# A fused attention kernel in which query products, one unit's additions and the probability spread change engines or form

## The reference, cut to what matters

```python
x = x + L0(gn(x))      # gn: group norm over 32 groups of 4 channels
x = x + L1(gn(x))

# L0: four dilations (1, 2, 4, 8), 32 channels and 2 heads each
q, k, v = split(w_qkv @ x)                          # per dilation i
attn = softmax(sum_d q * unfold3x3(k, dil) * scale) # over 9 neighbours
o = sum_9(attn * unfold3x3(v, dil))
out = concat(o_i * gate_i)     # gate: softmax of a linear layer on pooled x

# L1: 4 heads of 32 channels; p = W_qkv @ x + b, q = k = v = p
att = softmax(p_h @ p_h.T * scale)
out = W_proj @ (att @ p_h) + b_proj
```

## Time and profile before

| | us |
|---|---|
| median of three runs | 90.77 |
| lowest, highest | 90.47, 90.90 |
| span of the profiled execution | 88.6 |

### The profile page before, as it was taken

One profiled execution on the slowest core, in us unless ns is written; L12 is line 12 of the kernel. 1 busy time (PEld: TensorE's weight loads), 2 busy tenths in 40 slices (PEclk: granted clock), 3 DMA queues, 4 the chain that ended last, 5 costly groups with the idle time before them and its releaser, 6 DMA issues.

```text
span 88.6 us, 2254 instructions
## 1 busy us (share of the span) xinstructions
PE 71.5 (81%) x896; PEld 55.5 (63%) x896; DVE 74.1 (84%) x193; ACT 33.9 (38%) x104; POOL 45.6 (52%) x82
## 2 busy tenths in 40 slices
PE   0299997999967899295998799995998098999970
PEld 0299784576425797193988677794876054766840
DVE  1278399999999969999699888999999959875990
ACT  4496699063650000000018333040695036367220
POOL 7404585068000199793999998699992000600000
PEclk9999999999999999999999999999999858999999
DMA  1992013000000000000000000000000000003145
GB/s 24 326 360 62 0 33 64 0 0 7 0 0 4 4 7 0 0 0 0 4 7 0 0 0 0 0 0 7 0 0 7 0 0 4 0 0 118 43 145 174
DMA packets 3019, 3.11 MB, mean 35 GB/s; under 512 B 320, under 2 KB 2752, under 8 KB 3008
## 3 DMA queue, kind: packets, MB, share of 16 engines
q1 hardware_dynamic: 2576, 2.69, 9.6%
q10 hardware_dynamic: 432, 0.26, 1.3%
HBM read 1.91 MB, written 1.05 MB: 33 GB/s over the span
## 4 chain that ended last, share of the span: by engine, by line
DVE 45%; PE 28%; POOL 12%; issue 5%; ACT 4%; DMA 4%; DVEq 0%; ACTq 0%
PE ps L818 27%; DVE qk L615 22%; DVE pv L665 10%; POOL pv L368 6%; POOL acc L368 6%; DMA xt<-x_dram 4%; DVE acc L677 3%; DVE pv L677 3%; DVE ssum L632 1%; PE ps L954 1%; DVE x L710 1%; ACT pT L445 1%; DVE acc L665 1%; DVE x L684 1%; DVE smax L622 1%
## 5 line engine op out<-in xcount | busy, mean ns | idle before, releaser
L818 PE MATMUL ps<-prob,sel 128*128 128x180 f32 (+6 forms) x120 | 18.7, 309 | 4.8 <-DVE pv L665 3.6
L818 PEld LDWEIGHTS ps<-prob,sel 128*128 128x128 f32 x120 | 17.0, 190 | 6.9 <-DVE pv L665 5.1
L615 DVE TENSOR_TENSOR qk<-q,k 128x128 f32<-128x128 f32 (+7 forms) x36 | 21.1, 650 | 0.1
L665 DVE TENSOR_TENSOR pv<-ps,v 128x128 f32<-128x128 f32 (+7 forms) x32 | 17.1, 568 | 2.4 <-PE ps L818 2.0
L368 POOL TENSOR_TENSOR pv<-pv 128x240 f32<-128x240 f32 (+3 forms) x24 | 16.2, 682 | 2.0 <-DVE pv L665 1.8
L818 PE MATMUL ps<-xn,wp 128*32 128x256 f32 (+1 forms) x208 | 16.4, 382 | 0.1
L368 POOL TENSOR_TENSOR acc<-acc,pv 128x256 f32<-128x256 f32 (+4 forms) x20 | 13.2, 664 | 0.5
L333 POOL TENSOR_TENSOR rstd<-gvar,mhalf 128x2 f32<-128x2 f32 (+1 forms) x6 | 4.9, 824 | 15.4 <-DVE gvar L563 15.3
L818 PEld LDWEIGHTS ps<-xn,wp 128*32 128x32 f32 (+1 forms) x208 | 9.8, 116 | 4.4 <-ACT xn L452 0.6
L423 ACT ACTIVATE expd<-shifted 128x576 f32<-128x576 f32 x2 | 1.4, 683 | 21.3 <-DVE shifted L625 21.3
L818 PE MATMUL ps<-xt 128*128 128x128 f32 x28 | 5.9, 382 | 3.9 <-DMA xt<-x_dram 3.9
(11 more groups left out here) (81 smaller groups left out, 104.2 us busy)
## 6 DMA issues: line engine op xcount, KB each, us to landing
xt<-x_dram SPq DMA_DIRECT2D x4, 256.0 KB, 3.5
out_dram<-x SPq DMA_DIRECT2D x8, 128.0 KB, 1.8
wp<-wpack_dram SPq DMA_DIRECT2D x1, 325.0 KB, 5.3
sel<-selc_dram SPq DMA_DIRECT2D x4, 64.0 KB, 3.9
cs<-consts_dram ACTq DMA_DIRECT2D x1, 130.0 KB, 3.5
cs<-consts_dram ACTq DMA_DIRECT2D x2, 64.0 KB, 2.6
```

What stands on the lines that cost most here:

```text
L615: last = nc.vector.tensor_tensor(o, a, b, ALU.mult)
L665: last = nc.vector.tensor_tensor(o, a, b, ALU.mult)
L818: return nc.tensor.matmul(o, w, m, start=start, stop=stop)
```

## The change: what it does

- The query products of units (0,2), (1,2) and (1,3) are made by GpSimd, in the order (0,2), the gates' arithmetic, (1,2), (1,3), then the additions. The other five stay on VectorE. Of these, (0,1), (0,3), (1,0) and (1,1) read the queries from PSUM, where the projection left them in bank 2 or 3 (`Q_BANK`); ScalarE copies 20 tiles instead of 24, and three banks serve the copied ones.
- Every spread is float32 with weights of 64 rows: images 0 and 1 read rows 0 to 63, images 2 and 3 rows 64 to 127, in the order 0, 2, 1, 3. The bfloat16 parts, their steps and the `sel16` matrix are gone.
- Unit (0,3) is summed by TensorE: nine pieces accumulate in PSUM with an identity of 32 rows and columns. `restore` becomes `sum_units`, which sums by tiles of 32 × 32, all four images of a phase together. GpSimd adds units 0 to 2 of phase 0 and 0 and 1 of phase 1.
- The order of VectorE's, TensorE's and ScalarE's lists follows these; GpSimd's roots move to after the fourth and the sixth addition of (1,0), and `keep_clock` no longer waits for the softmax.

```diff
-POOL_SUMS = (ND, 2)
-RSQRT_AFTER = ((1, 0, 4), (1, 1, 0))
+POOL_SUMS = (3, 2)
+TENSOR_SUMS = ((3,), ())
+RSQRT_AFTER = ((1, 0, 3), (1, 0, 5))
...
-        PROJ_BANKS = (0, 1, 2, 3, 6)
+        PROJ_BANKS = (0, 1, 6)
+        Q_BANK = {(0, 1): 2, (0, 3): 3, (1, 0): 2, (1, 1): 3}
+        DVE_PRODUCTS = [(0, 0), (0, 1), (0, 3), (1, 0), (1, 1)]
+        POOL_PRODUCTS = [(0, 2), (1, 2), (1, 3)]
...
+            def multiply_qk(ph, s):
+                pool.wait_ge(proj_copied, max(copied_by(0, s, ph), copied_by(1, s, ph)))
+                if ph:
+                    pool.wait_ge(scores_ready, s + 1)
+                for ci in range(3):
+                    for o, a, b in query_operands(ph, s, ci):
+                        last = nc.gpsimd.tensor_tensor(o, a, b, ALU.mult)
+                last.then_inc(pool_qk_ready, 1)
...
-                for j in range(4):
+                for j in (0, 2, 1, 3):
                     i0, i1 = row_offsets(s, j)
                     o = view(ps, 1024 * (c % 2) + 64 * QR * j + W * i0 + c0, dims(W, 64))
-                    for n in range(3 if split else 1):
...
-                        last = mm(o, w[:, j, s, :], m, start=(n == 0), stop=(n == 2 or not split))
+                    half = 64 * (j // 2)
+                    m = view(prob, (ph * KK + 3 * ci + i0) * QP + c0, dims(QP, W), half, 64)
+                    last = mm(o, sel[half:half + 64, j % 2, s, :], m)
...
+            def sum_units(ph, units):
...
+                for n in range(max(len(part) for part in parts)):
+                    for s, part in zip(units, parts):
...
+                        for j in range(SLOTS):
+                            rows = slice(32 * j, 32 * j + 32)
+                            last = mm(view(ps, 512 * (BANK[2 * ph] + j) + r0 * W + c0, dims, 32 * s, 32),
+                                      ident[rows, rows], view(t, offset + r0 * W + c0, dims, 32 * j, 32),
+                                      start=(n == 0), stop=(n == len(part) - 1))
...
-            keep_clock(2, 1)
-            keep_clock(3, 1)
-            for i in range(2):
+            keep_clock(3)
+            for i in range(3):
                 spread(1, 0, i)
-            restore(0)
-            spread(1, 0, 2)
-            spread(1, 1, 0)
+            sum_units(0, (3,))
+            for i in range(2):
+                spread(1, 1, i)
+            sum_units(0, (0, 1, 2))
+            spread(1, 1, 2)
+            spread(1, 2, 0)
             group_stats(0)
...
-            restore(2)
-            restore(3)
+            pe.wait_ge(pv_ready, 12 * PHASES)
+            keep_clock(3, BANK[2])
+            sum_units(1, (0, 1, 2, 3))
```

More of the change, by code:

```diff
@@ L264, in batch, with copied_by, query_operands, neighbours @@
             return group(g).start + PHASES * i
-        tiles = []
-        for ph in range(PHASES):
-            tiles += [(kind, s, ph) for s in range(ND) for kind in (0, 1)] + [(2, s, ph) for s in range(ND)]
+        tiles = [(kind, s, 0) for s in range(ND) for kind in (0, 1)] + [(2, s, 0) for s in range(ND)]
+        tiles += [(kind, s, 1) for s in (0, 2, 1, 3) for kind in (0, 1)] + [(2, s, 1) for s in range(ND)]
+        copied = [(kind, s, ph) for kind, s, ph in tiles if kind or (ph, s) not in Q_BANK]
+        def copied_by(kind, s, ph):
+            return copied.index((kind, s, ph)) + 1
+        def query_operands(ph, s, ci):
+            c0, c1, co = columns(DIL[s], ci)
+            for n, ri, dri, r0, dr, a0, da, rows in pieces(s):
+                o = view(qk[s], (3 * ci + ri) * N + r0 * W + c0, [[dri * N + dr * W, n], [W, rows], [1, c1 - c0]])
+                in_psum = (ph, s) in Q_BANK
+                first = 512 * Q_BANK[ph, s] if in_psum else (s * PHASES + ph) * N
+                a = view(ps if in_psum else q, first + r0 * W + c0, [[dr * W, n], [W, rows], [1, c1 - c0]])
+                b = view(k[s], (ph * ROWS[s] + a0) * W + c0 + co, [[da * W, n], [W, rows], [1, c1 - c0]])
+                yield o, a, b
         def of_phase(ph):
             return slice(ph, B, PHASES)
+        def neighbours(s):
+            return [(3 * ci + ri, *valid_rows(s, ri), *columns(DIL[s], ci)[:2])
+                    for ci in CENTRE_FIRST for ri in CENTRE_FIRST]
+        def added_before(ph, s):
+            return len([u for u in range(POOL_SUMS[ph], s) if u not in TENSOR_SUMS[ph]])
         def operands(ph, s, n, target, slot):
@@ L477, in _ @@
             first_norm(6)
-            for n in range(4):
+            for n in range(3):
                 copy_tile(n)
@@ L652, in multiply_pv @@
                 if chunk == 0:
-                    dve.wait_ge(proj_copied, tiles.index((2, s, ph)) + 1)
+                    dve.wait_ge(proj_copied, copied_by(2, s, ph))
                 dve.wait_ge(spread_ready, c + 1)
-                if ph and chunk == 0:
+                if ph and chunk == 0 and s in TENSOR_SUMS[0]:
+                    dve.wait_ge(restored, SLOTS)
+                elif ph and chunk == 0:
                     dve.wait_ge(added, ADDS * (s + 1))
@@ L660, in multiply_pv @@
                     o = view(pv[s], (3 * ci + ri) * N + r0 * W + c0, [[dri * N + dr * W, n], [W, rows], [1, nc_]])
-                    if ci == 1 and n == 1:
+                    if ci == 1 and n == 1 and s not in TENSOR_SUMS[ph]:
                         o = view(acc, (ph * ND + s) * N, [[W, rows], [1, nc_]])
@@ L898, in spread @@
                     pe.wait_ge(sel_loaded, 64)
-                    pe.wait_ge(proj_copied, len(tiles))
+                    pe.wait_ge(proj_copied, len(copied))
+                if c == 1:
+                    pe.wait_ge(qk_ready, len(DVE_PRODUCTS))
                 if c >= 2:
                     pe.wait_ge(pv_ready, c - 1)
-                split = ph == PHASES - 1 and s > 0
-                if split and s == 1 and chunk == 0:
-                    pe.wait_ge(sel16_ready, ND - 1)
-                    for n in range(3):
-                        pe.wait_ge(part_ready[n], 1)
                 c0, c1, _ = columns(DIL[s], ci)
-                for j in range(4):
+                for j in (0, 2, 1, 3):
                     i0, i1 = row_offsets(s, j)
```

206 lines of the change are left out of this document (90 added, 116 removed).

## The result

| | before | after |
|---|---|---|
| median, us | 90.62 | 93.38 |
| lowest, highest | 89.67, 90.90 | 92.63, 94.57 |
| span of the profiled execution | 88.6 | 92.0 |

The ratio is 1.028, with a 95% interval of 1.019 to 1.036: the change makes the kernel slower, by 1.9 to 3.6%. Forecast was 85.2 us, faster. The page of the changed kernel: busy shares, granted clock in 40 slices.

The account below looks back on a forecast made before the run. The prediction took a chain to bound the kernel: VectorE, GpSimd's additions, VectorE alternating with TensorE, then the second layer's short dependent steps. 88.6 − 4.4 − 1.2 = 83.0 us of span, plus 2.2 gives 85.2 us; range 82.6 to 89.0 us.

Parts of the forecast that it names:

- the sum's term for the clock: TensorE between 30 and 60 us: taken to keep the full clock it has now, with no loss in the sum.
- case (c): Rival, chance 0.14: TensorE does less, so its clock falls in more stretches; one costs some 1.5 us, giving 86.7 us.
- part 5: Tail after the additions: last first-layer residual 3.2 us after them instead of 4.4, gain 1.2 us, remaining 13.6 us unchanged.
- part 1: Query products: 9.1 us leave VectorE, 3.4 us of it lost turns; GpSimd takes 12 us; probabilities lose 0.5 us.
- part 3: From 29.6 us to phase 1's first product with v: 15.4 us instead of 21.9, gain so far 6.5 us.
- part 4: Phase 1 up to the end of the additions: 21.2 us, 2.1 more than now, leaving a gain of 4.4 us.
- case (b): Rival, chance 0.09: row halves of the spreads do not overlap, 1.3 us a chunk, giving 94.4 us, slower than before.
- the price of the half-height spread: Phase 0 chunks, the main unknown: 0.64 us at 192 columns, 0.44 at 64, plus 0.3 us until the semaphore is seen.
- Its last term: End of the sum: 2.2 us of work around the instructions, added to the 83.0 us span to give 85.2 us.
- Part 2: Up to the first product with v: first softmax step at about 21.5 us, product at 29.5, gain 0.1 us.
- Case (a): Rival, chance 0.20: weight loads of the two halves follow one another, 0.86 us a chunk, giving 87.4 us.
- The remaining 13.6 us: Rest of the tail after the last first-layer residual: claimed to stay at 13.6 us.

Follow-up runs that it names:

- three repairs: Changed kernel with 14 phase-0 fillers, GpSimd waiting for phase 0's probabilities before unit (1,3), and roots after (1,1)'s fourth and fifth additions: median 86.03 us, ratio 0.924.
- the first experiment: Changed kernel plus 14 full-height filler matmuls in phase 0, 4 before the first chunk of unit (0,2) and 10 before its last: 90.07 us, ratio 0.991.
- the last experiment: Changed kernel with 14 phase-0 fillers, GpSimd's wait and later roots, plus twelve phase-1 fillers, six before (0,3)'s sum: 86.51 us, ratio 0.963.
- the first experiment's repeat: Changed kernel with the same 14 fillers of 128 rows in phase 0, run again beside the 64-row fillers: 89.64 us, ratio 0.992.
- its two variants above: Kernel before with half-height float32 spreads alone, median 89.94 us; kernel before with products of (1,2) and (1,3) reading a PSUM operand, 87.89 us, ratio 0.968.

## Why the prediction was wrong

**The sign.** The step that failed is the sum's term for the clock, which is nothing: it keeps TensorE at full clock wherever the kernel before had it, and case (c) gave one more stretch of 3.4 us a chance of 0.14 and a price of 1.5 us. The clock fell for two stretches of 10.2 us. The first cost 2.7 us, shown by the fillers, and with the fillers in place the ratio is 0.991 and 0.992 instead of 1.028. The tail lost about 2.3 us more, an estimate given under part 5. That is some 5.0 of the 9.0 us of span. The other 4.0 are the held-up step (1.45 in the first stretch, part 1), waits of phase 0 (0.9, part 3), the roots (1.2, part 4) and 0.5 of the tail. The question on which the forecast and case (b) stood on two sides, the price of the half-height spread, was answered as forecast.

That the version with three repairs has a median of 86.0 us, 0.8 from the forecast, is luck in part. It has 14 more fillers, later roots and a wait of GpSimd that the forecast kernel has not; in its profile the tail is 3.1 us longer than forecast, and the other stretches make up for some of it, 85.4 against 83.0 us of span. Its runs reach from 83.0 to 87.8 us.

**The sum.** Its last term is too large. Of the runs whose own span is listed, nearly all took 1.7 to 1.9 us more than it; the 2.2 us were the median of three runs less the span of another execution.

**Part 1, right in size, with one step wrong.** GpSimd's products took 4.36 us for (0,2) and 7.36 for the other two, 11.7 against 12. VectorE's five remaining units kept their length. The step that failed is "0 to 0.8 us each, 0.5 us taken in all" for the probabilities: 2.87 us instead of 0.82, and 1.24 in the second phase. I had taken as upper bound that the step doubles, by the products beside additions. The bound that held is another: the time from the step's start to the end of GpSimd's row of products (25.76 to 28.00 us), plus 0.6 us. In the first experiment's two profiles, with the same work beside it, the step took 1.24 and 1.23 us, in three others 2.71, 2.73 and 2.88, and 0.82 is had by keeping GpSimd away.

**Part 2, right.** The first softmax step began at 20.83 us (21.5 forecast), and without the hold-up 8.04 us follow it, where the forecast had 8.0.

**Part 3, right in its main unknown.** One chunk of 192 columns alone took 0.92 us and two 1.49 to 1.53, so 0.6 us each and 0.3 until the end is seen: 0.64 and 0.3 were forecast. Case (a), 0.86 with loads one after another, is out. Weight loads at full clock, half height (28 to 36.6 us of the changed kernel) and full height (33.9 to 36.6 us of the run with spreads of full height): count, busy time, mean ns of one.

```profile
L785 PEld LDWEIGHTS ps<-prob,sel 64*128 64x128 f32 x48 | 3.6, 186 | 4.4 <-DVE prob L622 2.9 <-DVE qk L602 0.8 <-DVE pv L645 0.5
```
```profile
L785 PEld LDWEIGHTS ps<-prob,sel 128*128 128x128 f32 x16 | 2.4, 190 | 0.2 <-issue 0.2
```

One load lasts as long in half height as in full, 186 and 190 ns, but 48 of them fit into 3.6 us, 0.075 us each, against 0.15. The rule weighed, from the Trainium skill, "TensorE: Matmul & The Clock Gate", section LDWEIGHTS, says that the time of one load goes with its columns and not its rows; these two lines agree. It does not bar two halves from loading together, and they did. With the clock held this stretch took 16.36 us against 15.5: VectorE's waits of 1.28 us at the change of phase (1.0 forecast) and 1.04 ahead of (0,1,0) (0.8), and the second probabilities' 0.4. The 2.7 us above that are the clock.

**Part 4, the order right and one bound missed.** The sum of (0,3) took 1.95 us (1.7), its wait 1.88 (1.6), the bias wait 1.26 (1.4), GpSimd's idle time 5.84 (4), the eight additions 5.6 (5.0). I costed the misplaced roots and took them as given, though the price stood in my own text: 1.4 us for the bias and 1.4 for the additions, 2.8 together. Moving them to the later place gave 4.0, and the 18.4 us that are left are the forecast's 21.2 less those 2.8; so the roots were under-priced by 1.2 us, the whole miss of this stretch.

**Part 5, wrong.** The last first-layer residual ended 3.9 us after the additions, not 3.2 (and 4.2 before, not 4.4): VectorE waited for the sums, which at half clock took 1.17 instead of 0.7 us:

```profile
73.83 0.42 DVE L664 SCALAR_TENSOR_TENSOR x<-ps,xt 128x256 f32<-128x256 f32 x1 [0.65 <-PE ps L785]
```

At full clock (the last experiment) the sums took 0.71, but they began 0.7 us after the last addition, behind the three fillers, and the wait was 0.78. In the first experiment's repeat, with the clock full up to there, the residuals ended 3.4 us after the additions. The remaining 13.6 us "stay" was wrong too: they became 15.7, as the clock stood at half up to 81.8 us, where the kernel before had it back at 73.8. In three profiles this part is 13.8 us long: the kernel before and its two variants above. In all three the clock was full in it, but for the last 1.1 us at most. In the changed kernel and its variants, with spreads of either height, it took 14.8 to 16.1 us, each time with a stretch at half clock in it. By this the clock costs the tail 15.7 less 13.8 and 3.9 less 3.4, together 2.3 us (an estimate: no run has the changed kernel with its clock full through the tail). Even with the clock full up to 71.5 us (the last experiment) the tail was 19.0 us, with VectorE waiting 2.22 us at the second layer's last scores, behind projections at half clock, where the kernel before waited 1.01. So the gain of 1.2 us showed in no profile: their tails were 18.4 to 20.0 us, and 18.0 before.

**Still open.** What decides where the clock falls is not shown. The runs show that the places differ between executions of one kernel (the first experiment at 68.3 us in one profile, at 57.0 in the other; the three repairs with a mean clock of 0.92 to 0.996), and that fillers held it in phase 0 and, the last time, in phase 1. It also stays open why VectorE's step gets its turn in one execution and not in another.

## What to carry to other kernels

When a change takes work from the engine that is near the bound, look at what the others now do in the gaps: a TensorE that is left with less work may lose half its clock, and every such gap belongs in the sum with a price, not as one rival. The price depends on what else the path waits for: in phase 1, 6.8 us at half clock cost 2.1 us with the roots late, and nothing with them early. When work goes to GpSimd, list every VectorE step with two SBUF operands that now lies beside it, allow for its being held until GpSimd's row of instructions ends, and move GpSimd, not the step. And place what GpSimd computes for others behind the work that can run meanwhile.

## What the runs showed of the hardware

- Two row halves of 64 rows load and multiply together: eight float32 records of 192 columns in 0.6 us, against 1.35 in full height (2.71 us for sixteen). One load of 128 columns lasted 186 ns over 64 rows and 190 over 128.
- 28 filler records over 64 rows held the clock as 28 over 128 rows did, in a place where without them it fell for 10.2 us.
- A step of VectorE that reads SBUF twice took 0.82 us alone and 1.24 or 2.71 to 2.88 us beside the same GpSimd work; in the long cases it ended 0.6 us after the last of GpSimd's products, which were not slowed.
- GpSimd's tiny operations are stretched too. The same addition of the gate arithmetic, first before, beside VectorE's query products from two SBUF operands, then after, where VectorE ended a product with a PSUM operand 0.1 us into it and then stood idle:

```profile
20.42 0.65 POOL L354 TENSOR_TENSOR gpick<-gpick 128x4 f32<-128x4 f32 x1
```
```profile
19.94 0.20 POOL L360 TENSOR_TENSOR gpick<-gpick 128x4 f32<-128x4 f32 x1
```
